# Two chained cross-attention layers on one core: key writes later in the queue, maxima's rows ahead of the key stacks, context loads issued by ScalarE, the layer norm counted in the planned list

## The reference, cut to what matters

```python
# layer 0
q = x @ Wq + 2 * (x @ Aq @ Bq);  k, v = the same from ctx, 8 heads each
attn = softmax(q k^T / 4);  x = x + lora_linear(attn v, Wo, Ao, Bo)
# layer 1
Q = x @ Wq.T + bq;  K = ctx @ Wk.T + bk;  V = ctx @ Wv.T + bv    # 32 heads
attn = softmax(where(mask, Q K^T / 4, -inf))
x = x + (attn V) @ Wo.T + bo
out = (x - mean) / sqrt(var + 1e-5) * ln_g + ln_b
```

## Time and profile before

| what | value |
|---|---|
| median of 3 runs | 1794.09 us (1790.18 to 1795.79) |
| the profiled execution | 1793.7 us, of which the span is 1791.9 us |
| TensorE matmul busy | 1691.4 us (94%) |
| VectorE, ScalarE, GpSimd busy | 1257.1, 1022.8, 186.7 us |
| granted TensorE clock, mean | 0.968 |

### The profile page before, as it was taken

One profiled execution on the slowest core, in us unless ns is written; L12 is line 12 of the kernel. 1 busy time (PEld: TensorE's weight loads), 2 busy tenths in 40 slices (PEclk: granted clock), 3 DMA queues, 4 the chain that ended last, 5 costly groups with the idle time before them and its releaser, 6 DMA issues.

```text
span 1791.9 us, 43738 instructions
## 1 busy us (share of the span) xinstructions
PE 1691.4 (94%) x18340; PEld 1198.1 (67%) x18340; DVE 1257.1 (70%) x2743; ACT 1022.8 (57%) x1880; POOL 186.7 (10%) x268
## 2 busy tenths in 40 slices
PE   6699999899979999999999999999999999999996
PEld 3567666576646766565677777777777776777662
DVE  1667777666757878786776667778777777777761
ACT  0046666555645666565655555665666665666563
POOL 2010212001220001111211100001000001000101
PEclk9789999899989999999999999999999999999998
DMA  7831335303351223335335246334353444344210
GB/s 196 252 69 29 75 75 157 59 20 66 84 156 33 48 29 66 66 66 162 66 68 93 49 76 145 51 48 70 46 124 50 58 58 118 56 58 58 44 28 12
DMA packets 65029, 138.12 MB, mean 77 GB/s; under 512 B 12540, under 2 KB 49436, under 8 KB 64832
## 3 DMA queue, kind: packets, MB, share of 16 engines
q1 hardware_dynamic: 64832, 135.33, 37.1%
HBM read 97.84 MB, written 34.89 MB: 74 GB/s over the span
## 4 chain that ended last, share of the span: by engine, by line
PE 87%; DMA 4%; DVE 3%; ACT 2%; SPq 2%; issue 2%; POOL 1%; POOLq 0%; ACTq 0%
PE value L918 21%; PE ring L875 13%; PE work L806 12%; PE work L826 12%; PE score L900 8%; PE score L895 8%; PE work L851 3%; PE work L949 3%; PE ring L863 2%; PE work L834 2%; DMA k_stack<-k_dram 1%; DMA q_stack<-few_rows 1%; ACT p_sb L984 1%; SPq L1353 1%; PE ring L928 1%
## 5 line engine op out<-in xcount | busy, mean ns | idle before, releaser
L984 ACT ACTIVATE p_sb<-score 124x512 f32<-124x512 f32 (+1 forms) x1664 | 932.9, 598 | 645.4 <-PE score L895 334.7
L1084 DVE TENSOR_REDUCE chunk_max<-ring 128x1 f32<-128x402 f32 x2048 | 1056.0, 569 | 211.2 <-PE ring L875 198.7
L875 PE MATMUL ring<-k_stack,q_stack 64*128 64x402 f32 x2048 | 776.2, 453 | 27.6 <-issue 9.7
L918 PE MATMUL value<-p_sb,v_sb 124*32 124x256 f32 x6656 | 423.3, 388 | 0.4 <-ACT p_sb L984 0.4
L875 PEld LDWEIGHTS ring<-k_stack,q_stack 64*128 64x128 f32 x2048 | 358.2, 188 | 93.1 <-DVE chunk_max L1084 36.0
L895 PE MATMUL score<-q_stack,k_stack 64*124 64x512 f32 (+1 forms) x832 | 381.3, 511 | 19.6 <-DMA q_stack<-few_rows 17.2
L900 PE MATMUL score<-q_stack,k_stack 64*124 64x256 f32 (+1 forms) x1664 | 366.2, 320 | 8.5 <-DMA q_stack<-few_rows 6.2
L826 PE MATMUL work<-wv,ctx_sb 64*124 64x128 f32 x3840 | 367.1, 278 | 2.3 <-ACT v_sb L1006 1.0
L826 PEld LDWEIGHTS work<-wv,ctx_sb 64*124 64x124 f32 x3840 | 337.2, 186 | 12.0 <-PE work L826 4.6
L806 PE MATMUL work<-ctx_sb,wk 64*128 64x402 f32 x1280 | 308.9, 518 | 7.9 <-DMA ctx_sb<-ctxT 7.1
L918 PEld LDWEIGHTS value<-p_sb,v_sb 124*32 124x32 f32 x6656 | 189.4, 110 | 160.5 <-issue 52.4
(11 more groups left out here) (67 smaller groups left out, 573.6 us busy)
## 6 DMA issues: line engine op xcount, KB each, us to landing
k_stack<-k_dram SPq DMA_DIRECT2D x288, 200.1 KB
k_dram<-k_parts SPq DMA_DIRECT2D x60, 402.0 KB, 2.6
ctx_sb<-ctxT SPq DMA_DIRECT2D x24, 992.0 KB, 6.2
k_dram<-k_parts SPq DMA_DIRECT2D x20, 395.0 KB, 2.9
q_stack<-few_rows SPq DMA_DIRECT2D x256, 2.0 KB
wq<-l_Wq SPq DMA_DIRECT2D x2, 1024.0 KB, 11.6
xt_sb<-xT SPq DMA_DIRECT2D x4, 512.0 KB, 11.0
wo<-l_Wo SPq DMA_DIRECT2D x2, 1024.0 KB, 6.4
```

The costliest lines, as they stand in the source:

```text
L875: engine.matmul(ring[bank_of["max", u, half, m]][:, 0:MW], q_stack[rows, u % 3, j, q * P:(q + 1) * P], k_stack[rows, 2 * (z % 3) + (u % 2 ...
L918: done = engine.matmul(value_bank[32 * j:32 * j + 32, 0:S], v_sb[0:tn, seq % 2, i, head * VW:head * VW + 32], p_sb[0:tn, (2 * n + j % 2) % ...
L984: engine.activation(p_sb[0:tn, n % PLACES, :], score_bank[n % 2][0:tn, :], ACT.Exp, scale=SCALE).then_inc(s_exp, 1)
L1084: engine.tensor_reduce(chunk_max[:, u % 2, half, m // NM, m % NM:m % NM + 1], ring[bank_of["max", u, half, m]][:, 0:MW], AX.X, ALU.max)\
```

## The change

Five things are edited. The DMA that writes a key part (`write k`) becomes a step of its own, which `read` puts on a list `writes`; it is appended to the program three tiles later (`write_keys`), or earlier if a `stack` or another key product comes. The step `stack` of unit u + 2 is appended only once `turn m` of unit u is in the list (`load_stack`), and `max_open` looks at `stacked`. The context loads after the first batch's are issued by ScalarE, at their place in the list, and the plan counts 450 ns for each in `scalar_free`. The steps of the layer norm are appended after every second score, and each adds to `vector_free` what `NORM` says. Since the plan's sums differ, its choices differ from unit 7 on.

```diff
     def step(self, *name):
+        if name[0] == "stack":
+            self.write_keys(None)
         self.steps.append(name)
+
+    def write_keys(self, now):
+
+        while self.writes and (now is None or self.writes[0][0] <= now):
+            self.steps.append(self.writes.pop(0)[1])
...
         if kind == "k":
+            self.write_keys(None)
...
                 self.step("read k", name[1], c)
+                self.writes.append((self.now + 3, ("write k", name[1], c)))
...
                     self.step("load ctx", z + 1, c)
+                    self.scalar_free += 450
...
-        return unit < self.UNITS and unit <= self.at_unit + ahead and ("turn q", unit) in self.emitted and \
+        return unit < self.UNITS and unit <= min(self.stacked, self.at_unit + ahead) and ("turn q", unit) in self.emitted and \
...
+        if kind == "turn m" and self.next_stack == name[1] + 2:
+            self.load_stack()
...
-            self.step("stack", u + 2)
+            self.next_stack = u + 2
+            if ("turn m", u) in self.emitted:
+                self.load_stack()
...
+    def load_stack(self):
+
+        self.step("stack", self.next_stack)
+        self.stacked, self.next_stack = self.next_stack, None
...
                 self.score(s, half)
                 s, half = s + half, 1 - half
-                self.norm()
+                if half:
+                    self.norm()
...
+    NORM = {"sums": 950, "variance": 200, "root": 0, "centre": 620, "inverse": 200, "normalise": 550}
+
     def norm(self):
         if self.slow:
-            self.step(*self.slow.pop(0))
+            name = self.slow.pop(0)
+            self.vector_free = max(self.vector_free, max(self.free) - 1000) + self.NORM[name[0]]
+            self.step(*name)
...
         def scalar(engine):
...
+                elif kind == "load ctx":
+
+                    z, c = a
+                    user = plan.ctx_after[z, c]
+                    e.wait_ge(s_made[user[0]], made[user])
+                    load_ctx(engine, z, c)
...
-                elif kind == "read k":
+                elif kind == "write k":
```

More of the change, by code:

```diff
@@ L53, in __init__ @@
         self.ctx_now, self.ctx_since, self.chunk_product = [0] * NC, [0] * NC, [None] * NC
-        self.todo = []
+        self.todo, self.writes = [], []
+        self.stacked, self.next_stack = 1, None
         self.prologue()
@@ L465, in score @@
         self.budget += self.plan_rate() / 2
+        self.write_keys(s)
     def burst(self, issued, at):
@@ L967, in tensor, with load_ctx @@
                     done.then_inc(s_made["turn mask"], 1)
+        def load_ctx(engine, z, c):
+            lo, hi = chunk(c)
+            engine.dma_start(ctx_sb[:, :, lo:hi], ctxT[z % B].rearrange("(k p) t -> p k t", p=P)[:, :, lo:hi])\
+                .then_inc(s_ctx[c], 16)
         def scalar(engine):
@@ L1249, in load_lora @@
                 engine.dma_start(lora_b[:, s * H:s * H + widths[n]], w0[f"B{n}"]).then_inc(s_w[f"b{s}"], 16)
[L1251 to L1257, removed]
             def load_xt(b):
@@ L1266, in sync @@
             engine.dma_start(wk0[:, :, :], by_tile(w0["Wk"])).then_inc(s_w["wk0"], 16)
-            load_ctx(0, 0)
+            load_ctx(engine, 0, 0)
             load_lora("q")
@@ L1271, in sync @@
             for c in range(1, NC):
-                load_ctx(0, c)
+                load_ctx(engine, 0, c)
             engine.dma_start(wv0[:, :, :], by_tile(w0["Wv"])).then_inc(s_w["wv0"], 16)
@@ L1307, in sync @@
                     engine.dma_start(wq[:, :, :], by_tile(w1["Wq"])).then_inc(s_w["wq1"], 16)
-                elif kind == "load ctx":
-                    load_ctx(*a)
                 elif kind == "load xt":
                     load_xt(a[0])
-                elif kind == "read k":
+                elif kind == "write k":
                     seq, c = a
```

## The result

The changed kernel takes 1811.6 us (median of 4 executions, 1807.8 to 1812.8) against 1794.9 us of the kernel before: a ratio of 1.0095, with a 95% interval of 1.0077 to 1.0113. It is slower by some 17 us, where 1795 us was forecast and the range ended at 1808.

The account below looks back on a forecast made before the run. The prediction took TensorE as the bound, its matmuls busy for 1691.4 of 1791.9 us (94%). Its terms, +0.1 + 6 + 3 - 9 + 1 = +1.1 us on 1793.7, gave 1795 us, range 1780 to 1808.

Parts of the forecast that it names:

- The layer norm: VectorE's norm sums delay reductions; spreading the steps was to save 4 us idle and 5 us of clock.
- Context loads on ScalarE: 24 loads issued ahead of ScalarE's readings of products; +3 us taken, bounds 0 and 12.1 us.
- The order by itself: TensorE's new list: fewer value-product bursts, fewer score-maximum pairs in opposite halves; +1 us, within -2 and +8.
- the fourth rival: The norm gains nothing, since its VectorE time is unchanged and sums still block reductions; 1804 us, chance 0.13.
- Rows ahead of stacks, writes later: SyncE's queue and the turns of maxima: old waits go, new ones come at other units; +0.1 us in sum.
- Stacks: Key-stack waits of 4.5 and 2.7 us stay, a new one comes at unit 18; +4 us and 2 us of clock.
- The turns that were listed as added: New turns right ahead of units 11, 15, 18, 44, 51 and 62: 17.3 us of waits, plus 10 us of clock.
- Unit 18's stack: Key stack at unit 18, late once unit 16's stall goes: +4 us and 2 us of clock, bounds 0 and 7 us.
- the mark of a wrong step: Sign that the forecast is wrong at that step: TensorE's waits for ScalarE pass 10 us.
- the third rival: ScalarE's context issues pass to TensorE in full, with clock dips at units 7, 15 and 27; 1811 us, chance 0.15.
- the first: Rival: key stacks land sooner because contexts no longer go first, at units 10 and 18; about 1781 us, chance 0.17.

Follow-up runs that it names:

- norm_moved: Changed kernel with the steps of the three norms inside the run moved to later tiles, TensorE's order kept: 1806.8 us, ratio 1.0065.
- rk_norm: Kernel before plus three queue edits, norm's edit and 4300 ns counted from turn to first score, no charge for context loads: 1772.6 us, ratio 0.9889.
- norm_only: Kernel before with the norm's edit alone, queues as before and no charge for context loads: 1813.1 us, ratio 1.0113.
- all_uncharged: Kernel before with the three queue edits (contexts by ScalarE, writes later, stacks behind the turn), TensorE's order of before: 1783.1 us, ratio 0.9942.
- no_norm: Changed kernel without the norm's edit, all other edits kept, including 450 ns per context load: 1794.5 us, ratio 1.0006.
- queue_only: Kernel before with key writes later and stacks behind the turn, contexts still issued by SyncE, TensorE's order of before: 1787.4 us, ratio 0.9949.
- ctx_act_uncharged: Kernel before with only the contexts issued by ScalarE, nothing charged in the plan: 1791.5 us, ratio 0.9989.

## Why the prediction was wrong

The step that failed is "The layer norm": it was put at -4 us idle and -5 us of clock, and its edit costs +17 us in the changed kernel (1794.5 to 1811.6) and +19 us alone. A second one failed in the same way: "Context loads on ScalarE" took the plan's 450 ns as a help ("puts other work there"), and they cost 11.4 us (1783.1 to 1794.5), 8.4 of them at unit 45, while the queue edits brought 10.6 us. Together: -10.6 + 11.4 + 17.1 = +17.9 us, from the 1793.8 us of the kernel before beside these runs to 1811.6. Both act through the order, and for that "The order by itself" had +1 us and at most +8.

- The part of the norm's term that was named came true in direction: the waits for reductions fell from 8.6 to 3.5 us. What I did not price is what else stands in VectorE's order: the sums ahead of the copy of a turned row. I gave unit 51's turn 3.5 us, by the matmuls in between; it took 6.42. norm_moved took that wait to 4.90 and the time down by about 5 us.
- The norm's square root brings two table loads on ScalarE, before and after the change. Before, the score behind them waited 0.27 us:

```profile
1235.44 1.28 ACT L1028 ACT_TABLE_LOAD   x1
...
1236.95 1.28 ACT L984 ACT_TABLE_LOAD   x1
...
1238.90 0.28 PEld L900 LDWEIGHTS score<-q_stack,k_stack 64*124 64x124 f32 x1 [0.27 <-ACT p_sb L984]
```

With the steps spread over more tiles, TensorE waits 2.18 us for the exponential behind them:

```profile
1220.05 1.28 ACT L1067 ACT_TABLE_LOAD   x1
...
1221.56 1.28 ACT L1017 ACT_TABLE_LOAD   x1
...
1223.51 0.77 PE L928 MATMUL score<-q_stack,k_stack 64*113 64x256 f32 x2 [2.18 <-ACT p_sb L1017]
```

There are three of these (2.18, 1.63, 2.20 us), 6.0 us that no term of the sum held. They take back the 5.1 us won at the reductions. The 5 us of clock weren't won either: the trace has the clock at half for 13.7 us at the norms before (from 1233.0 and 1693.8 us on) and for 13.7 us at these three waits after (from 1223.2, 1451.9 and 1704.5 us on). So at the norms themselves the edit gains nothing, as the fourth rival held. No run took the table loads away alone, and rk_norm, which has them too, loses nothing by the norm's edit.
- What remains of the 17 us comes with the order. In norm_only, where only this edit is in, unit 44 waits 9.14 us and unit 62 3.01 us where neither waited a whole microsecond before. Which half of the edit does it, the places of the steps or their cost in `vector_free`, was not tried.

"Rows ahead of stacks, writes later" was right in what it gave to the queue and too low in the price. In all_uncharged the order is the old one: unit 13's wait is gone, unit 16's is 3.12 us, and units 10 and 25 still wait 3.78 and 2.20, as said. But 10.6 us are won, since unit 28's wait for its key stack is gone too and unit 8's is 2.66 us instead of 4.52. "Stacks" held that neither would go away; in the changed kernel both are gone, and TensorE's waits for the DMAs of `k_stack` are 5.1 us instead of 8.4. At unit 10 the turn stands nine scores ahead of the first of its unit, farther than the two tiles told above, and the wait is gone. The turns that were listed as added came where I said and as long as I said, unit 51 apart: units 11, 15, 18, 44, 51 and 62 with 1.21, 2.77, 3.81, 3.91, 6.42 and 2.75 us, 20.9 together against 17.3 of the sum.

Unit 18's stack was late next, as said, by 2.1 us and not 4, within the bounds. The clock was not hurt there.

"Context loads on ScalarE": the issue costs 0.41 us each at the median, inside the 0.4 to 0.6 forecast. The issuing by itself is a gain or nothing (0.9989). But TensorE waited 17.3 us for exponentials in the changed kernel instead of 3.8, over the 10 us that I had set as the mark of a wrong step; 6.0 of them are the norm's above. Three others (297.6, 515.4 and 809.5 us: 1.82, 1.63 and 2.08) stand at the three-load places, as the third rival says, though no dip of the clock follows them. They stand in no_norm too, which takes the time of before, and in part in all_uncharged (2.07 us at 812.0), which is faster. So they are a cost of some 5 us, which the queue edits pay back, and not what makes the changed kernel slower than these two.

"The order by itself" at +1 us was the worst-founded term: a count of bursts and pairs says nothing of what stands beside what. The order also moved the last use of a context next to a key stack when the 450 ns were charged (8.4 us at unit 45 of no_norm). I had looked in the new list for turns next to scores, and not for context loads next to stacks.

Of the rivals, the fourth, on the slower side, has the right edit and too small a price: it held that the norm gains nothing, where it costs 17 us. Of the first (stacks sooner, since the queues take turns): the contexts' own queue hardly protected what landed beside them. At unit 16, with the same order of issues, 3.9 us passed from the rows' last issue to the score with the contexts on ScalarE's queue (all_uncharged, 517.31 to 521.21) and 4.3 us with them on SyncE's (queue_only, 516.36 to 520.62). In rk_norm the rows of 1088.87 and two chunks issued at 1089.39 by ScalarE went together, and the score waited 4.21 us:

```profile
1088.87 2.48 SPq L1387 DMA_DIRECT2D q_stack<-few_rows  x4
...
1089.39 1.01 ACTq L1004 DMA_DIRECT2D ctx_sb<-ctxT  x2
...
1098.81 0.54 PE L933 MATMUL score<-q_stack,k_stack 64*124 64x256 f32 x1 [4.21 <-DMA q_stack<-few_rows]
```

From the last issue (1091.35) to the score it is 7.5 us, as with one queue at unit 16 before, and not 1.2. By the Trainium skill, page "DMA: Bandwidth & Descriptors", section "Queues, rings and completion order", each DMA engine takes turns between queues packet by packet. The trace does not contradict that, but taking turns with a context was hardly faster than standing behind it. Section "Issuing engines are not separate DMA queues" of that page of the Trainium skill, that issuing from another engine saves only sequencer time, fits ctx_act_uncharged (0.9989).

What stays open: how the 17 us of the norm's edit divide between the turns, the table loads and the pairs of halves side by side, since every run that mends one of them by way of the plan gets a new list.

## What to carry to other kernels

A planner that writes an order by its own costs is as good as the latency that it doesn't know: here 4.3 us from a transpose over a copy and four small DMAs to the first user counted as nothing, and a new charge elsewhere moved that gap to a place where it hurt. Price such a chain in the plan first, and only then refine the costs of the rest. That is not enough by itself: the norm's edit did no harm once the chain was priced, but the 450 ns, close to the 0.41 us that an issue takes, still cost 9.9 us, of which 3.3 are a wait at a stack with two loads beside it, another thing that the plan knew nothing of. When a list changes, look in the new one for each pair that must not be neighbours (a turn and its first user, a large load and an urgent one, a side job and an urgent copy), on every engine.

## What the runs showed of the hardware that was not expected

A small transfer issued from one engine is held up by a large one from another engine nearly as much as by one in its own queue: 3.9 against 4.3 us to use at unit 16 with the same order of issues, and 7.5 us beside two chunks (rk_norm at unit 38), against 1.2 us with the DMAs at rest. Moving 2 loads of 992 KB by two tiles was worth 8.4 us at one place. And the clock's price does not go by the wait's length alone: after the wait of 6.42 us it was at half for 8.4 us and, after one more wait of 1.63 us, for another 3.4; after the one of 8.89 us before, for 6.3 us and then full; and after waits of 1.82, 1.63 and 2.08 us at units 7, 15 and 27 of the changed kernel it did not fall at all.
